# A fused attention and FP4 feed-forward layer: down weights transposed through two PSUM banks, and a new order of the weight steps and of the turn

## What is computed

```python
x = L0_attn_x
xn = _layernorm(x, axis=-1)
s = _L0_attn_ref(xn, L0_attn_Wq, L0_attn_Wk, L0_attn_Wv, L0_attn_Wo)
g = _silu(_L0_ffn_ref(xn, L0_ffn_w_gate, L0_ffn_w_up, L0_ffn_w_down))
x = x + s * g
```

## Time and profile before

| | |
|---|---|
| median of 3 runs | 552.62 us (551.38 to 553.28) |
| the profiled execution | 552.81 us, its span 551.0 us |
| PE busy | 487.9 us (89%), 4962 matmuls |
| DVE, ACT, POOL busy | 434.0, 401.3, 431.1 us (79, 73, 78%) |
| granted TensorE clock, mean | 0.947 |

### The profile page before, as it was taken

How to read it: one execution, slowest core, us unless ns; L and a number is a source line. 1 busy time by engine, 2 the same in 40 slices (tenths; PEclk the granted TensorE clock), 3 DMA queues, 4 the chain that set the end, 5 groups by cost and what they waited for, 6 DMA issues and landing times. The chain is left out here.

```text
span 551.0 us, 13894 instructions
## 1 busy us (share of the span) xinstructions
PE 487.9 (89%) x4962; PEld 413.6 (75%) x4962; DVE 434.0 (79%) x848; ACT 401.3 (73%) x572; POOL 431.1 (78%) x941
## 2 busy tenths in 40 slices
PE   0335659999999999999999999999999999998975
PEld 0223538888888888888888888888888888887765
DVE  5887756888888888888888888888888888887552
ACT  3136546888888888888887888888888888888721
POOL 7786963788888888888887888888888888877521
PEclk9756858999999999999999999999999999999997
DMA  8111020122232223222131113222222122221000
GB/s 308 45 39 28 12 76 1 40 49 50 50 87 49 50 50 87 49 49 49 44 83 34 32 45 87 49 51 49 49 49 51 49 50 49 49 49 43 8 21 19
DMA packets 78037, 29.36 MB, mean 53 GB/s; under 512 B 67472, under 2 KB 77456, under 8 KB 77968
## 3 DMA queue, kind: packets, MB, share of 16 engines
q1 hardware_dynamic: 77680, 28.38, 19.7%
q10 hardware_dynamic: 288, 0.08, 0.1%
HBM read 7.49 MB, written 4.19 MB: 21 GB/s over the span
## 5 line engine op out<-in xcount | busy, mean ns | idle before, releaser
L944 ACT ACTIVATE probs<-scores 128x1024 f32<-128x1024 f32 (+1 forms) x128 | 128.3, 1003 | 25.8 <-PE scores L389 21.2
L1075 POOL TENSOR_SCALAR_AFFINE_SELECT probs<-probs 128x512 f32<-128x512 f32 x128 | 82.2, 643 | 23.1 <-ACT probs L944 20.0
L1082 POOL TENSOR_SCALAR_AFFINE_SELECT probs<-probs 128x512 f32<-128x512 f32 x120 | 76.4, 636 | 0.0
L465 PE MATMUL bank_b<-probs,vals 128*32 128x128 f32 x1984 | 60.8, 274 | 3.0 <-DVE att L679 1.0
L427 PE MATMUL gt<-wdn_hi,hT_hi 128*128 128x256 f32 x192 | 61.1, 318 | 0.6 <-DVE xT_lo L582 0.6
L465 PEld LDWEIGHTS bank_b<-probs,vals 128*32 128x32 f32 x1984 | 53.0, 110 | 10.7 <-DVE vals L666 8.9
L1108 POOL TENSOR_TENSOR h_q<-h_grid,h_scale 128x704 f32<-128x704 bf16 x32 | 44.3, 1385 | 21.1 <-DVE h_grid L617 21.1
L952 ACT ACTIVATE gate<-gt 128x704 f32<-128x704 f32 x32 | 24.2, 757 | 43.2 <-PE gt L276 43.2
L427 PE MATMUL gt<-wdn_lo,hT_hi 128*128 128x256 f32 x192 | 54.8, 285 | 0.0
L427 PE MATMUL gt<-wdn_hi,hT_lo 128*128 128x256 f32 x192 | 54.6, 284 | 0.0
L389 PE MATMUL scores<-qk_slots 48*128 48x256 f16 x480 | 47.3, 276 | 3.0 <-ACT probs L944 3.0
(11 more groups left out here) (146 smaller groups left out, 1584.1 us busy)
## 6 DMA issues: line engine op xcount, KB each, us to landing
x_all<-x SPq DMA_DIRECT2D x8, 512.0 KB, 4.0
out<-y SPq DMA_DIRECT2D x32, 128.0 KB, 1.7
x_all<-wproj SPq DMA_DIRECT2D x1, 768.0 KB, 6.8
dn_raw<-wd SPq DMA_DIRECT2D x1, 704.0 KB, 8.5
probs<-wg SPq DMA_DIRECT2D x1, 640.0 KB, 5.2
probs<-wu SPq DMA_DIRECT2D x1, 640.0 KB, 7.2
qk_slots<-qk_stack SPq DMA_TRANSPOSE x32, 3.7
x_all<-wproj SPq DMA_DIRECT2D x1, 256.0 KB, 8.7
```

The costliest lines, as they stand in the source:

```text
L465: done = e.matmul(bank_b[32 * n:32 * n + 32, grp * P:(grp + 1) * P], va, pr, start=part == 0, stop=part == 1 or final(i))
L944: e.activation(probs[j % P_BUFS][:, grp, :, side(j), :], sc[:, :, :, side(j), :].rearrange("p b e h q -> p (b e) h q"), ACT.Exp).then_inc( ...
L1075: e.affine_select(out=own, in_=own, compare_op=ALU.is_ge, fill=0.0, base=0, pattern=[[0, GRP], [-1, P]], channel_multiplier=1).then_inc(s_ ...
L1082: e.affine_select(out=part, in_=part, compare_op=ALU.is_gt, fill=0.0, base=0, pattern=[[0, GRP], [1, P]], channel_multiplier=-1).then_inc( ...
```

## The change

It does five things. The down weights' three transposed groups go through `bank_b`, `bank_a`, `bank_b` instead of `bank_b` alone. The TensorE loop is turned round: what was the end of turn t (scores 3, back, the last down parts, wo, qk, v) is now the head of turn t+1, `tr_h` stands behind the first half of up, and scores 3 ahead of back and wo. The gate and up transposes begin in turn 0 (groups 0 and 1), and the down transposes are spread over turn 2 (one ahead of `tr_x(3)`, one behind the first half of up) and the head of turn 3. The steps on VectorE, ScalarE and GpSimd are put in a new order as well, both the weight steps and those of every turn. No instruction is added to or taken from the computation.

The core of the diff (`+` is the kernel after):

```diff
-        WD_GROUPS = [0, 2, 4]
+        WD_GROUPS, WD_BANKS = [0, 2, 4], [bank_b, bank_a, bank_b]
...
+                elif n == 1:
+                    e.wait_ge(s_silu, WD_TURN - LAG + 1)
                 else:
-                    e.wait_ge(s_lo_wd, n)
-                transposes(bank_b, [wd_rows[:, r, k * P:min(k * P + P, FF)] for k in (k0, k0 + 1)
-                                    for r in range(2)]).then_inc(s_tr_wd, 1)
+                    e.wait_ge(s_lo_wd, n - 1)
+                transposes(WD_BANKS[n], [wd_rows[:, r, k * P:min(k * P + P, FF)] for k in (k0, k0 + 1)
+                                         for r in range(2)]).then_inc(s_tr_wd, 1)
...
                 elif f >= 1:
-                    e.wait_ge(s_silu, f)
+                    e.wait_ge(s_lo_wd, 2)
                 product(gt_all[:, H0:512], xT[t % 2], KT, wgu, 0, HALF)
...
             tr_x(0)
-            qk_mm(0)
-            v_mm(0)
-            for t in range(END):
+            for t in range(END + 1):
                 f, g = t - LAG, t - LAG - 1
+                if exists(t - 2):
+                    scores(t - 2, 3)
+                if exists(t - 4):
+                    back(t - 4)
+                if exists(g - 1):
+                    down_mm(g - 1, 4, FT)
+                if t == 3:
+                    tr_wd(2)
+                if exists(t - 5):
+                    wo_mm(t - 5)
+                if t >= 1 and exists(t):
+                    qk_mm(t)
+                    v_mm(t)
                 if exists(f):
                     gate_mm(f)
                 if exists(t - 1):
                     scores(t - 1, 0)
...
                 if exists(t - 3):
                     pv(t - 3)
-                if exists(g):
-                    tr_h(g)
+                if t == WD_TURN:
+                    tr_wd(0)
+                if t == 1:
+                    tr_wgu(2)
+                if t == 0:
+                    qk_mm(0)
+                    v_mm(0)
                 if 0 <= t + 1 < X_TURNS:
                     tr_x(t + 1)
                 if exists(f):
                     up_mm(f)
+                if t == 1:
+                    tr_wgu(3)
+                if t == WD_TURN:
+                    tr_wd(1)
+                if t == 0:
+                    tr_wgu(0)
+                if exists(g):
+                    tr_h(g)
...
-                if t == 1:
-                    tr_wgu(3)
+                if t == 0:
+                    tr_wgu(1)
+                if t == 1:
+                    tr_wgu(4)
+                    tr_wgu(5)
                 if exists(g):
                     down_mm(g, 0, 4)
...
-                if t == WD_TURN:
-                    for n in range(len(WD_GROUPS)):
-                        tr_wd(n)
```

More of the change, by code:

```diff
@@ L710, in lo_wd @@
             def lo_wd(n):
-                k0 = WD_GROUPS[n]
+                k0, b = WD_GROUPS[n], WD_BANKS[n]
                 e.wait_ge(s_hi_wd, n + 1)
@@ L767, in vector_program @@
             lo_wproj(1)
+            scales_w(1)
+            scales_w(2)
+            ln_moments(2)
             round_w(0)
-            scales_w(1)
-            amax_x(0)
-            wide_x(0)
-            rscale_x(0)
-            norm_x(0)
-            squares(0)
-            norm_w(2)
-            for t in range(END):
-                f = t - LAG
+            norm_w(2)
+            for t in range(END + 1):
+                f, g = t - LAG, t - LAG - 1
+                if t == WD_TURN:
+                    lo_wgu(4)
+                    lo_wgu(5)
+                if t == 3:
+                    lo_wd(2)
+                if t == 1:
+                    lo_wgu(0)
+                if t == 0:
+                    rscale_x(0)
+                if exists(f - 1):
+                    norm_h(f - 1)
+                if exists(t - 4):
+                    attend(t - 4)
+                if t == 3:
+                    lo_wo()
+                if exists(t - 5):
+                    gated(t - 5)
+                if exists(f - 1):
+                    up_h(f - 1)
+                if t == 0:
+                    squares(0)
+                    round_w(2)
+                if t == 1:
+                    scales_w(WD_SCALES)
+                    lo_wgu(1)
                 if exists(t):
                     values(t)
+                if t == WD_TURN:
+                    round_w(6)
+                if exists(f - 1):
+                    grid_h(f - 1)
+                if t >= 1 and exists(t):
+                    squares(t)
+                if t == WD_TURN:
+                    lo_wd(0)
                 if t == 0:
-                    scales_w(2)
-                    round_w(2)
+                    norm_x(0)
                 if exists(t + 3):
                     ln_stats(t + 3)
-                    ln_moments(t + 3)
-                if t == 1:
-                    lo_wgu(0)
-                    lo_wgu(1)
+                if exists(t + 1):
+                    amax_x(t + 1)
                 if exists(t):
@@ L796, in vector_program @@
                     norm_x(t + 1)
-                if exists(t - LAG - 1):
-                    lo_h(t - LAG - 1)
-                if t == 1:
-                    lo_wgu(2)
-                if exists(t):
-                    unit(t)
+                if t == WD_TURN:
+                    lo_wd(1)
                 if t == 0:
@@ L1016, in scalar_program @@
                 if t == 1:
-                    hi_wgu(4)
                     hi_wgu(5)
-                if exists(g):
-                    down_silu(g)
-                if t == 0:
-                    square_w(6)
                 if exists(t + 1):
                     square(t + 1)
-                if t == 0:
-                    square_w(7)
-                    hi_wo()
-                if t == WD_TURN:
-                    for n in range(len(WD_GROUPS)):
-                        hi_wd(n)
+                    square_x(t + 1)
+                if exists(f + 1):
+                    silu(f + 1)
+                if t == 1:
+                    hi_wd(0)
+                if t == 0:
+                    hi_wgu(2)
+                if exists(t):
+                    exp(t, 0)
+                if 0 <= t + 2 < X_TURNS:
+                    hi_x(t + 2)
+                if exists(t - 2):
+                    keep_pv(t - 2)
+                if exists(g + 1):
+                    hi_h(g + 1)
+                if t == 0:
+                    hi_wgu(3)
+                    square_w(7)
+                if t == 1:
+                    hi_wd(1)
+                if exists(t):
+                    exp(t, 1)
+                if t == 1:
+                    hi_wo()
+                if exists(g + 1) or exists(g):
+                    hi_tail(g + 1)
+                if exists(t):
+                    exp(t, 2)
+                if exists(t + 1):
+                    hi_q(t + 1)
+                if t == 0:
+                    hi_wgu(4)
+                if exists(t + 1):
+                    hi_k(t + 1)
+                if t == 1:
+                    hi_wd(2)
+                if exists(t):
+                    exp(t, 3)
         def gpsimd_program(e):
```

210 lines of the change are left out of this document (84 added, 126 removed).

## The result

| | before | after |
|---|---|---|
| median of 4 runs | 552.13 us (551.38 to 553.28) | 531.55 us (530.18 to 533.70) |
| profiled execution, its span | 552.81, 551.0 us | 533.70, 532.0 us |
| mean granted clock | 0.947 | 0.962 |

The ratio is 0.9629, 95% interval 0.9591 to 0.9668: 20.6 us less. The forecast was 540.8 us, 535.5 to 548.0; the direction was right, the gain too small, by 9.3 us. In the profiled executions the span fell by 19.0 us.

What follows compares the result with a forecast made beforehand. PE bounds the steady part, VectorE 20 to 40 us, waits 40 to 80 us. Four start stretches, -1.3 - 3.7 + 0.6 - 7.6 = -12.0 us, from 552.81 give 540.8 us; range 535.5 to 548.

Steps and rivals of the forecast that it cites:

- A: Start of the kernel to qk(1): two waits and x steps of tile 0 leave VectorE's list; -1.3 us.
- the end: Last tile's chain through rounding, down, attention and store: same steps, 0 us, half a us to each side.
- the steady turn: Each repeating turn: same matmuls and number of changes of kind on PE; 0 us, 0.1 us to each side.
- The low end given: Stretch to qk(1): -3.8 us if no VectorE division ran beside a GpSimd instruction.
- The other reading of A: Stretch to qk(1): moved divisions each wait for a whole GpSimd instruction; nearer +1 than -1.3 us.
- B: qk(1) to qk(2): scores of tile 0 no longer wait 4.06 us for an exp; -3.7 us.
- C: qk(2) to qk(3): gate(0)'s wait goes, lot 6 rounding and down groups come in; +0.6 us.
- D: qk(3) to gate(1): two banks and earlier groups remove the down transpose block ahead of v(3); -7.6 us.
- The clock: Rival: fewer gaps put PE at 2.4 GHz from qk(3) on; some 4 us more gain, 536.8 us; chance 0.14.
- The blocked queue: Rival: in turn 2 tr_wd(0) waits for lots 6 and 7, blocking PE; about 5 us, 546 us; chance 0.16.
- the longer turn: Rival: v(t) or scores 3 waits in every steady turn; at 0.6 us a turn 557 us; chance 0.08.
- a lo_qk row that PE waits for: Sign that the forecast is wrong, looked for in the trace's steady turns; no size given.

Runs made afterwards that it cites:

- the run with one bank: The changed kernel with all three down transpose groups back in one bank, in a row between qk(3) and v(3): 539.33 us, ratio 0.9753.
- the two start-and-turn runs: New order up to turn 4, then the order of before: 535.59 us, 0.9697; order of before up to turn 4, then the new: 547.51 us, 0.9914.
- values late: The changed kernel with values(t) moved back on VectorE behind grid_h and squares(t) from turn 4 on: 538.28 us, ratio 0.9745.
- unit early: The changed kernel with unit(t) back ahead of lo_x on VectorE from turn 4 on: 560.00 us, ratio 1.0143.

## Why the forecast was too high, by its own steps

The steps that failed are three terms of the sum: A at -1.3 us (measured -4.0), and two that stood at nothing, the speed at which gate(1) runs (-1.3) and the end (-1.6). In the steady turn two effects were missed that nearly cancel.

- **A, -1.3 forecast, -4.0 measured.** The waits that fell away, 0.97 and 0.47 us, and x_amax and x_wide came as forecast. What the sum had no term for is the time of VectorE's instructions beside GpSimd; it was only in the ends of the range. From the second lo_wproj to lo_qk the four divisions took 4.35 us before (1.48, 1.25, 0.42, and 1.20 at 31.78, a row that the prediction did not use) and 2.45 after (0.86, 0.41, 0.43, 0.75), and with them grid_x fell from 1.16 to 0.42 us and the first lo_wproj from 1.60 to 0.95. Against that, two small scale steps took 0.86 and 0.98 us (17.29 in the rows) for 0.19 and 0.24. These rows and the waits make some 3.9 of the 4.0 us. The 0.6 us charged for new waits did not come: VectorE runs without a gap from 13.3 to 32.4 us. Of the four divisions only norm_w(2), at 20.88, meets one of GpSimd's roundings (norm_x(0), at 25.14, stands beside the short steps of root); in the run that moved norm_x(0), three divisions that met GpSimd cost 0.4 to 1.0 us more each. The low end given, -3.8, was near, but the rows named beside it give only -1.9 - 1.1 - 0.55 = -3.55. The other reading of A, near +1 because each moved division would wait for a rounding, was wrong about the meetings: one of four came.
- **B, -3.7 and -4.05.** The right number for the wrong reason, which is luck. The scores' wait of 4.06 us (it is the fourth group of heads, waiting for the exp of the third) lay largely beside a longer chain: qk(1) to unit(1) took 13.2 us before and 10.2 after. Putting the exp back cost nothing in the new order. The lot 7 square and magic copy, charged at 0.4 us, stand ahead of exp 1 and make a new wait of 2.67 us (42.04), which also costs nothing, because unit(1) is still to come.
- **C, +0.6 and +0.5**: the sum agrees. Its parts were not measured one by one; the run with one bank shows that the down groups and their copies in turn 2 are 1.7 us of C, where rounding, groups and copies together were put at 2.7.
- **D, -7.6 and -7.8**: as worked out, and shown by the run with one bank.
- **The clock, a rival at 0.14**: partly true. qk(3) and v(3) still ran at the 1.2 GHz level, but gate(1) went over to 2.4 GHz at 68.1 us, after PE had been busy since 63.48, and its silu came 1.3 us earlier than the forecast had it. Before, all of gate(1) ran at the low level (granted clock 0.51 from 82.8 to 86.5 us).
- **The blocked queue, a rival at 0.16**: it did not come. GpSimd finished lot 7 at 48.22, and the first down transposes, at 54.09, waited 1.18 us for lot 6 on VectorE.
- **Steady turn, 0 with 0.1 either way.** -0.18 us for an undisturbed turn is outside that. I counted changes of kind on PE, and not the waits in the trace: pv waited for values in every turn, in plain sight in the view of waits. The margin of v behind attend did not grow from 0.58 to 1.0 us either: by turns it was 0.66 before and is 0.57 now. No wait came of it, so the longer turn, a rival at 0.08, stayed away, though not by the reason given. unit did have to move once values came early: ahead of lo_x it costs 1.1 us a turn.
- **What I left out**: the SP queue. I followed what is moved past what on VectorE, ScalarE and GpSimd, and missed that GpSimd's addition of x, and with it the store, goes from just behind y to behind root and q_x, and so to just ahead of the next transpose. Late transposes give back 4.7 us. The sign "a lo_qk row that PE waits for" came in this form: PE waits for the transpose behind lo_qk.
- **The end, 0 and -1.6**: the last two gates waited 2.7 us for y and ffn_gate before and 1.8 us after, and the two start-and-turn runs show that the new turn order brings the whole 1.6 us. What makes the rest of it was not looked into.
- **The sum.** A (-2.7 beyond forecast), clock (-1.3), end (-1.6), B (-0.35), turns (-0.4), and small ones make 7 us of the 19.0 against 12.0. The rest of the 9.3 us is that the median of after lies 2.1 us below its profiled execution. That its other runs had fewer late transposes would do it, but those runs have no trace, so it is not shown.
- **Terms do not add.** 2.0 us lost at qk(1) were 0.25 at silu(2), 1.5 lost at qk(2) were 0.4. Part of a delay of the early chain is caught up before silu(2), some of it by the earlier rise of the clock (67.7 for 68.1 us); where the rest goes is not shown. So A and B, undone alone, are worth less than the table says.

## What to carry to other kernels

An instruction moved in a rotation of several in-order queues is worth what all its neighbours do: values early was -0.16 us a turn together with the other moves of that list and +1.0 us alone. Before costing a steady turn at zero, read each engine's small recurring waits in the view of waits, and follow the queue of DMAs through the new phase too, because a store that keeps its place in the order can still come to lie right ahead of a transfer that PE waits for. A little slack ahead of the user (scores 0 behind pv, 1.9 us) was worth more, by the medians, than removing one cause of lateness (526.9 against 530.0 us, the two intervals just touch).

## What the runs showed of the hardware that was not expected

- A DMA transpose of the same size, on the same queue, issued in 1.3 to 1.8 us and landed in 3.6 to 3.9 us in the steady turns of the kernel before and of that with values late. All 36 transposes of these runs that stood less than 1.8 us behind an x load took 2.0 to 4.4 us to issue and landed in 4.2 to 6.5. With the load 2.5 us or more ahead (values late, unit early) they took 1.3 to 1.6.
- In most kernels one or a few transposes of the steady turns took 2.4 to 3.6 us with no x load near, with the store ahead of them 2.1 or 3.1 us or 11 to 13 us back. They come at similar times in kernels with the same spacing (165.5 to 165.6 us in four of them). The second transpose of the program, with nothing but another transpose ahead of it, 12.6 to 16.1 us back, took 2.7 to 3.5 us in all 13 kernels with the new start and 1.6 in all 7 with the old. No run explains these.
- VectorE's division with both inputs in SBUF took 0.41 us alone and 1.21 us begun under a GpSimd instruction; its rounding steps with one input in PSUM stayed at 0.68 to 0.70 us beside the same GpSimd work.
